# An attention and FFN block: the product with the values for two key blocks at once, in every second slot

## The reference

```python
scores = jnp.einsum('bhqd,bhkd->bhqk', q * scale, k)
scores = scores + position_bias * 8.0
attn = jax.nn.softmax(scores.astype(jnp.float32), axis=-1).astype(scores.dtype)
ctx_out = jnp.einsum('bhqk,bhkd->bhqd', attn, v)
```

## Time and profile before

| | |
|---|---|
| median of 3 runs | 3767.62 us |
| the profiled execution | 3775.49 us |
| its span | 3773.3 us |
| TensorE busy | 3451.7 us (91%) |
| VectorE busy | 3208.9 us (85%) |
| ScalarE busy | 1774.6 us (47%) |
| GpSimd busy | 1691.7 us (45%) |
| mean granted TensorE clock | 0.972 |

### The profile page before, as it was taken

One profiled execution on the slowest core, in us unless ns is written; L12 is line 12 of the kernel. 1 busy time (PEld: TensorE's weight loads), 2 busy tenths in 40 slices (PEclk: granted clock), 3 DMA queues, 4 the chain that ended last, 5 costly groups with the idle time before them and its releaser, 6 DMA issues.

```text
span 3773.3 us, 78735 instructions
## 1 busy us (share of the span) xinstructions
PE 3451.7 (91%) x22906; PEld 2026.9 (54%) x22906; DVE 3208.9 (85%) x7270; ACT 1774.6 (47%) x2776; POOL 1691.7 (45%) x1773
## 2 busy tenths in 40 slices
PE   1599999999999999999999999999999999999986
PEld 0245555555555555555555555555555555555555
DVE  7468888898888888888889888888888888888976
ACT  2255554444554444555444455444445544445441
POOL 2214544445444445454444544444445444454454
PEclk6799999999999999999999999999999999999997
DMA  3553323233323233332323332323333232333000
GB/s 98 95 82 71 64 62 58 49 73 75 73 55 62 58 59 73 72 68 58 64 44 72 76 73 57 61 55 61 72 73 66 59 63 45 73 75 67 20 22 12
DMA packets 199185, 237.18 MB, mean 63 GB/s; under 512 B 23424, under 2 KB 177568, under 8 KB 198736
## 3 DMA queue, kind: packets, MB, share of 16 engines
q1 hardware_dynamic: 198736, 231.64, 31.4%
HBM read 163.72 MB, written 67.31 MB: 61 GB/s over the span
## 4 chain that ended last, share of the span: by engine, by line
PE 60%; DVE 19%; issue 8%; DMA 5%; SPq 4%; ACT 2%; DVEq 1%; POOL 1%; ACTq 0%; POOLq 0%
PE ps_x L635 16%; PE ps_o L623 8%; PE rings L586 8%; PE rings L602 8%; PE ps_x L661 6%; DVE neg_max L980 5%; DMA x_in<-in_x 5%; SPq L480 3%; PE rings L605 3%; DVE x_in L1000 2%; PE rings L587 2%; PE rings L589 2%; DVE scale L1039 2%; PE ps_x L668 1%; PE ps_x L679 1%
## 5 line engine op out<-in xcount | busy, mean ns | idle before, releaser
L784 ACT ACTIVATE probs<-rings 128x1024 f32<-128x1024 f32 x1024 | 1049.3, 1025 | 1073.8 <-PE rings L589 1073.2
L980 DVE TENSOR_REDUCE neg_max<-rings 128x1 f32<-128x512 f32 x2048 | 1368.6, 679 | 202.2 <-PE rings L605 200.2
L602 PE MATMUL rings<-k_rows,q_rows 120*128 120x512 bf16 x2048 | 782.8, 387 | 31.2 <-DVE neg_max L980 19.6
L586 PE MATMUL rings<-q_rows,k_rows 121*128 121x512 bf16 x2048 | 730.0, 384 | 53.2 <-ACT probs L784 45.6
L623 PE MATMUL ps_o<-probs,values 128*32 128x512 f32 x4096 | 545.5, 605 | 0.9 <-ACT probs L784 0.9
L605 PE MATMUL rings<-band_m,rev 128*128 128x192 f16 (+1 forms) x2048 | 495.7, 242 | 0.0
L602 PEld LDWEIGHTS rings<-k_rows,q_rows 120*128 120x128 bf16 x2048 | 198.0, 97 | 519.4 <-DVE neg_max L980 292.5
L587 PE MATMUL rings<-band_t,rev 128*128 128x128 f16 x2048 | 451.5, 220 | 0.0
L1279 POOL TENSOR_TENSOR hidden<-hidden,inv 128x704 f32<-128x704 f32 x128 | 177.8, 1389 | 608.4 <-DVE inv L1043 608.4
L589 PE MATMUL rings<-band_t,rev 128*128 128x128 f16 (+1 forms) x2048 | 432.3, 211 | 0.0
L635 PE MATMUL ps_x<-w_gu_h,xq_h 128*128 128x512 f32 (+1 forms) x768 | 326.1, 425 | 27.7 <-DVE hq_l L1058 25.2
(11 more groups left out here) (180 smaller groups left out, 6808.2 us busy)
## 6 DMA issues: line engine op xcount, KB each, us to landing
parts_dram<-parts SPq DMA_DIRECT2D x128, 384.0 KB, 2.4
q_rows<-parts_dram SPq DMA_DIRECT2D x384, 128.0 KB, 4.4
k_rows<-parts_dram SPq DMA_DIRECT2D x384, 128.0 KB, 7.0
mod_rows<-mod_rows_dram SPq DMA_DIRECT2D x32, 640.0 KB, 4.9
x_in<-in_x SPq DMA_DIRECT2D x32, 512.0 KB, 8.9
x_mid<-in_x SPq DMA_DIRECT2D x128, 128.0 KB, 2.2
out<-x_mid SPq DMA_DIRECT2D x128, 128.0 KB, 1.7
probs<-in_wmod SPq DMA_DIRECT2D x1, 1536.0 KB, 7.6
```

Of the source, the lines that this page charges most:

```text
L586: mm(ps_s[:, bank, :], kr[0:ROW_MAX + 1, h, k0:k0 + P], qr[0:ROW_MAX + 1, h, :], start=True, stop=False)
L602: mm(ps_m[:, bank, :], q_rows[par][0:ROW_MAX, h, j * P:(j + 1) * P], k_rows[par][0:ROW_MAX, h, :], start=True, stop=False)
L784: A(prob_pair(s, j), ps_s, ACT.Exp).then_inc(exp_done, 1)
L980: v.tensor_reduce(neg_max[:, par, 4 * h + j:4 * h + j + 1], ps_m[:, (4 * h + j) % RING_M, :], AX.X, ALU.max, negate=True).then_inc(max_don ...
```

## The change

`weigh` is called in even slots only, and there does the units s - 2 and s - 1 one after the other, eight matmuls with one semaphore increment at the end. The probabilities get ten tiles in place of six: the four of odd units have their own places, even units alternate for the pair j = 0 as before and share one place for j = 2. The counts that ScalarE waits for are halved accordingly. The scratch in SBUF set aside for dynamic transfers becomes 8192 bytes, half of what it was.

```diff
-        probs = sb("probs", [P, 6, S])
+        probs = sb("probs", [P, 10, S])
...
+        def first_prob(unit, j):
+
+            if unit % 2:
+                return 6 + 2 * (j // 2)
+            return 4 if j >= 2 else unit % 4
+
         def prob(unit, j):
-
-            return probs[:, 2 * (unit % 2) + j if j < 2 else 2 + j, :]
+            return probs[:, first_prob(unit, j) + j % 2, :]
...
-                u = (s - 1) % 16
-                g, kb = u // 4, u % 4
-                wait(pe, exp_done, prev * 32 + 2 * (u + 1))
+                u = (s - 2) % 16
+                g = u // 4
+                wait(pe, exp_done, prev * 32 + 2 * (u + 2))
                 if u == 0:
                     after(pe, v_dve, prev, "v1")
-                if kb == 0:
+                if u % 4 == 0:
                     wait(pe, sum_copied, prev * 4 + g)
-                for j in range(G4):
-                    h = G4 * g + j
-                    m = mm(ps_o[32 * j:32 * j + 32, :], values[:, par, kb, h * VW:h * VW + 32],
-                           prob(u, j), start=kb == 0, stop=kb == NT - 1)
+                for unit in (u, u + 1):
+                    kb = unit % 4
+                    for j in range(G4):
+                        h = G4 * g + j
+                        m = mm(ps_o[32 * j:32 * j + 32, :], values[:, par, kb, h * VW:h * VW + 32],
+                               prob(unit, j), start=kb == 0, stop=kb == NT - 1)
                 m.then_inc(pv_done, 1)
...
-                        if j == 1:
+                        if j == 1 and s % 2 == 0:
                             weigh(it, s)
...
-                            if j == 0:
-                                wait(act, pv_done, n * 16 + (s - 1))
-                            if j == 2:
-                                wait(act, pv_done, n * 16 + s)
+                            wait(act, pv_done, n * 8 + (s // 2 - 1 if (s % 2, j) == (0, 0) else s // 2))
...
-                                wait(act, pv_done, ob * 16 + 4 * (og + 1))
+                                wait(act, pv_done, ob * 8 + 2 * (og + 1))
...
-    nc = bacc.Bacc("TRN2", target_bir_lowering=False, num_devices=1)
+    nc = bacc.Bacc("TRN2", target_bir_lowering=False, num_devices=1, dynamic_dma_scratch_size=8192)
```

More of the change, by code:

```diff
@@ L392, in build @@
         CR = slice(ROWS_QK, P)
+        def first_prob(unit, j):
+            if unit % 2:
+                return 6 + 2 * (j // 2)
+            return 4 if j >= 2 else unit % 4
         def prob(unit, j):
-            return probs[:, 2 * (unit % 2) + j if j < 2 else 2 + j, :]
+            return probs[:, first_prob(unit, j) + j % 2, :]
         def prob_pair(unit, j):
-            at = 2 * (unit % 2) if j < 2 else 4
-            return probs[:, at:at + 2, :]
+            return probs[:, first_prob(unit, j):first_prob(unit, j) + 2, :]
         def gate_up(w, kt, op, n0):
```

## The result

| | before | after |
|---|---|---|
| median of 4 runs each | 3766.7 us | 3831.32 us |
| lowest and highest | 3762.86, 3770.4 | 3829.51, 3832.17 |
| span of the profiled execution | 3773.3 us | 3829.9 us |
| mean granted TensorE clock | 0.972 | 0.965 |

The ratio is 1.0171, with an interval of 1.0153 to 1.0189: 64.6 us slower. 3813 was forecast, 3831.32 lies inside the range; 45 us of loss were forecast, the loss is 20 us larger. The time alone doesn't tell the cases apart: 3831 lies at the upper end of the forecast's own sum (3795 to 3832), and also inside the times given for more half clock (3822 to 3840) and for the dearer product (3826 to 3842). The rows and the experiments have to decide.

What follows compares the result with a forecast made beforehand. TensorE paces slots 6 to 14, a VectorE and DMA chain the rest. 28 iterations at 1.55 us longer make 43, with the ends 45, added to the median: 3813 us, eight-in-ten range 3760 to 3842.

Steps and rivals of the forecast that it cites:

- the forecast's own sum: Whole run: 1.0 to 2.2 us longer per iteration, 3795 to 3832 us; chance 0.58 for the forecast itself.
- more half clock: Rival: longer wait at xT0 brings half clock to the other half of iterations, 11 us, 3822 to 3840; chance 0.14.
- the dearer product: Rival: units of a pair still pay for each other, 2.1 to 2.18 us, 3826 to 3842; chance 0.08.
- The price of the pair: TensorE's doubled product: 1.98 us against 1.09 for a single one; a pair saves 0.20 us.
- The walk: One iteration from hT0 of slot 6: delays followed slot by slot; an iteration 1.6 to 1.9 us longer.
- The stops in slots 10 and 14: TensorE at hT0: waits for `context` of 0.86 us in slot 10 and 0.76 us in slot 14.
- The room at hT0: Slots 10 and 14: hT0 stands 0.23 and 0.33 us above the smallest distance from `context`; 1.09 are taken away.
- The rival without these stops: Hidden give in the chain behind g0 keeps hT0 from stopping: 3755 to 3772 us; chance 0.09.
- the one with TensorE alone: Rival: TensorE alone sets the time, all savings count, 45 to 51 us less, 3720; chance 0.11.
- the sign for the chain through SyncE: Load of `x_in`: must come later within the iteration than before, or the prediction is wrong; no size given.
- Busy and idle time: TensorE over the run: busy time about 50 us less, idle time about 100 us more.
- Parts at nothing: ScalarE's new waits, more tiles and the smaller scratch cost nothing; scratch 0, with 2 us either way.

Runs made afterwards that it cites:

- the runs that give hT0 its room back: VectorE divides `context` one position earlier, ahead of a reduce: on the kernel after 3786.49 us, ratio 1.0018; on the kernel before 3775.8 us, 0.998.
- the same line: The one-line move of VectorE's division of `context` from position 3 to 2; in the kernel before 3775.8 us, 0.998.
- the five matmuls: Five more small matmuls in the setup: kernel after 3813.8 us, 1.0109; after with `context` divided earlier 3766.47 us; before 3759.74 us; before with `context` divided earlier 3758.68 us.
- the kernel with `context` early: Kernel after with VectorE dividing `context` at position 2 in place of 3, ahead of one reduce: 3786.49 us, ratio 1.0018.
- the comparison of 0.9985 with 0.9973: Kernels after and before, both with `context` divided one position earlier and five more setup matmuls: 3766.47 us, 0.9985, and 3758.68 us, 0.9973.
- the fastest kernel: Kernel with pairs only in slots 0, 4, 8 and 12, `context` divided one position earlier and five more setup matmuls: 3741.7 us, ratio 0.993.
- the pair ahead: Kernel after with the doubled product at position 0 of even slots, ahead of maxima and hT0, in place of position 1: 3940.64 us, ratio 1.0447.
- even units alone: Kernel after without the second unit of each pair, odd key blocks left out of the product: 3712.06 us, ratio 0.9825.

## Why the prediction was right, and where it was short

**The price of the pair: right.** 1.98 was taken for the doubled product. The next matmul starts 1.86 behind its start, against 1.00: 0.86 for the second unit. With the 0.09 at its entry it is 1.95, and a pair saves 0.23. The rival that the pair saves nothing falls: rounds three and four issue their weights at 2123.97 and 2124.40, 0.43 apart, under running matmuls that use the same rows, and nothing is added. The page of the Trainium skill that spoke against it (TensorE: Matmul & The Clock Gate, "The mechanism" in Part 3: weights load under running matmuls only into other row groups) isn't borne out by these rows.

**The walk: right at each step.** The table has the medians of iterations 6 to 27 against before, in us from hT0 of slot 6, for even and odd iterations.

| place | forecast | measured |
|---|---|---|
| p1, slot 7 | -0.2 to +0.05 | -0.07, -0.11 |
| g0, slot 9 | +0.7 to +0.95 | +0.88, +0.82 |
| hT0, slot 10 | +0.45 to +0.7 | +0.65, +0.60 |
| g0, slot 13 | +1.15 to +1.4 | +1.27, +1.19 |
| hT0, slot 14 | +0.8 to +1.1 | +0.96, +0.86 |
| maxima behind the product, slot 14 | +1.7 to +2.0 | +1.86, +1.76 |
| VectorE's reduce, slot 14 | +1.6 to +1.9 | +1.75, +1.65 |

The stops in slots 10 and 14 were forecast at 0.86 and 0.76 and are 0.84 and 0.75. The room at hT0, 0.23 and 0.33 us read from the earlier trace rows, was the decisive reading, and the runs that give hT0 its room back show it as the cause. The rival without these stops is out, and so is the one with TensorE alone. The load of `x_in` starts later too, by 1.3 us in even and 2.0 in odd iterations, counted as in the table, so the sign for the chain through SyncE held.

**The average over iterations, and a term that was missing.** This is where the 20 us went. 1.55 us an iteration were taken, 28 times. Between iterations 3 and 28 the length is 113.3 us in place of 111.4, +1.89. The iterations ahead of those and the setup give 4.4 us in all, and the span's 56.6 us are 30 times 1.89, so 28 was a little low and 1.55 the more so. The missing term is the branch at the loop's end: 1.27 us longer, 12 times, 15 us. The delay of VectorE's reduce arrives whole at the last tile of slot 15 (+1.77 and +1.66). From there to the next hT0 of slot 6, on average over iterations 6 to 27, 0.39 us are lost again after even iterations, and 0.84 come in after odd ones, which end in the branch. The difference, 1.23 us, is about what the branch is longer. The prediction followed x_in and `context` into the next iteration and left out TensorE's own start.

The runs give the loss by cause, in shares of 64.6 us: 50 us are the stops at hT0 (58 less the 8 that the same line brings before; 49 with the five matmuls), and about 15 are the branch, if it counts in full as in the kernel with `context` early (12.4 us for 13.8 of branches). That leaves nothing for TensorE's saving of 0.23 us a pair, as in the comparison of 0.9985 with 0.9973. The part of the stops is measured twice; that of the branch is argued, and it isn't the only account: the five matmuls took 23 us from the kernel after, 9 more than its branches, and the kernel with pairs in slots 2, 6, 10 and 14 loses 62 us with short branches. From the spans' 56.6 to the medians' 64.6 us it is the profiled execution of before that makes the difference; it lay 8.8 us above its median, that of after 0.9.

**Busy and idle time: half right.** -50 and +100 were forecast, -12.9 and +70 came. The product lost 40 us (L623, 545.5, to L628, 505.4). Most of the rest was probably eaten by stretches at the half clock: counted between 300 and 3480 us, there were 14 of them, 48 us together, and there are 28, 106 us; 58 us more at half speed can take up to 29. Windows of after (length, busy us of TensorE, TensorE's weight loads, VectorE, ScalarE, GpSimd with their counts, PEclk, DMA share, GB/s): the first 5.77 us behind a branch, then the time after it.

```profile
2163.03:2168.80 5.77, 5.77 (x26) 1.78 (x26) 2.71 (x6) 1.37 (x2) 0.99 (x1) 0.50 0.65 118
2169.00:2174.80 5.80, 5.80 (x39) 4.16 (x38) 4.36 (x8) 3.39 (x5) 3.57 (x3) 1.00 1.15 138
```

PEclk 0.50 is the level of 1.2 GHz. It stands at the start of the iteration, after 2.78 us in which TensorE did nothing, and in slot 5, after xT0's wait that has grown from 2.05 to 2.67; these rows are of TensorE in after.

```profile
2087.51 1.11 PE L659 MATMUL ps_x<-ident,x_in 128*128 128x128 f32 x4 [2.67 <-DVE exp L1072]
...
2163.03 0.60 PE L589 MATMUL rings<-q_rows,k_rows 121*128 121x512 bf16 x1 [2.78 <-issue]
...
2165.38 3.58 PE L628 MATMUL ps_o<-probs,values 128*32 128x512 f32 x16
2168.89 0.39 PE L605 MATMUL rings<-k_rows,q_rows 120*128 120x512 bf16 x1
```

The doubled product takes 3.51 us there in place of 1.86. The rival "more stretches at the half clock" saw the one in slot 5 and gave it 11 us. It did come, and costs little: the kernel with `context` early has 29 stretches, 109 us, and a ratio of 1.0018. Both places lie by TensorE's wait at xT0, ahead of it and right behind it. No run changes the half clock alone, so what it costs beside the pairs' saving isn't measured.

**Parts at nothing: right.** More tiles, ScalarE's waits and the scratch: ratio 1.0001 for tiles and scratch. ScalarE's new counts ran only inside kernels with the pair; the kernel with pairs in slots 0, 4, 8 and 12 has such counts too and is faster than before, so nothing of size is in them, unless the pairs' saving hides it.

## What to carry to other kernels

In an order written out by hand, a block of work that depends on little is also cover between a job and the reader of its result: before it is merged with another or moved, read at every reader behind it how far it stands from the end of what it waits for, and compare with the smallest such distance in the trace. Room of 0.2 to 0.3 us against 1.09 us taken away turned a saving of 0.23 us a pair into a loss of 1.7%, of which 1.3% is measured at hT0. The same pairs in slots with room lost nothing (0.9985), and gained 0.4% in the fastest kernel. And at a loop's end, read the branch of the engine that paces it: a change of a few instructions elsewhere can move it by a microsecond.

## What the runs showed of the hardware

- TensorE's taken branch takes 3.5 to 3.7 us on average in some kernels and 4.7 to 4.85 in others, and five matmuls in the setup, outside the loop, change it. Means of the 12: before 3.58, before with `context` early 3.50, the kernel with more tiles 3.62, pairs in slots 2, 6, 10 and 14 3.63, the pair ahead 3.63, even units alone 3.66; after 4.85, after with `context` early 4.77, pairs in slots 0, 4, 8 and 12 4.67. All kernels with the five matmuls: 3.62 to 3.72. The one not taken takes 0.08. ScalarE's and GpSimd's branch on the same line takes 0.045 us at the most, with no such cost. I had not expected that the length hangs on anything but the loop. That the place of the code is the cause is inferred from the five matmuls; no run shows how.
- Weights of four column tiles, fp32 and in two passes, are loaded under the running matmuls over the same rows: the weights of rounds three and four are issued 0.43 us apart, and the second unit adds 0.86 us in all (1.86 in place of 1.00), 0.43 a round. The change of tile shape is paid once for the pair, 0.23 us less; the Trainium skill (TensorEngine Tiling (Array Packing), Key Properties) says that a change of tiling mode drains the engine, and these 0.23 us agree.
- With `context` early, the kernel after has 109 us at the half clock and the kernel before 41, and it takes 0.38% longer, 14 us. The 12 branches, 1.27 us longer each, come to 15. So 68 us more at the half clock leave no loss that these runs show, net of what the pairs save.
